# First feed-forward stage: input weights loaded and split first, every pair's front six chunks later, down products 12 chunks behind the up products

## The reference, cut to what matters

```python
xn = _layernorm(x, axis=-1)
gates = softmax(xt @ Wg.T); scores, inds = top_k(gates, 2); scores /= sum(scores)
g = einsum('td,ehd->teh', xt, We_gate)
u = einsum('td,ehd->teh', xt, We_up)
y_all = einsum('teh,edh->ted', silu(g) * u, We_down)
y = sum(take_along_axis(y_all, inds) * scores)
shared = silu(xt @ Ws_gate.T) * (xt @ Ws_up.T) @ Ws_down.T
y = y + sigmoid(xt @ Wsg.T) * shared
```

## Time and profile before

| what | us |
|---|---|
| median of three runs (lowest, highest) | 2506.7 (2501.7, 2507.82) |
| the profiled execution, its own time | 2507.11 |
| its span, first to last instruction | 2505.4 |
| TensorE busy (share of the span) | 2250.0 (90%) |
| VectorE busy | 1914.7 (76%) |
| ScalarE busy | 1736.3 (69%) |
| GpSimd busy | 843.7 (34%) |
| last instruction of the first stage | 424.5 |

### The profile page before, as it was taken

How to read it: one execution, slowest core, us unless ns; L and a number is a source line. 1 busy time by engine, 2 the same in 40 slices (tenths; PEclk the granted TensorE clock), 3 DMA queues, 4 the chain that set the end, 5 groups by cost and what they waited for, 6 DMA issues and landing times. The chain is left out here.

```text
span 2505.4 us, 90533 instructions
## 1 busy us (share of the span) xinstructions
PE 2250.0 (90%) x34464; PEld 1764.0 (70%) x34464; DVE 1914.7 (76%) x7571; ACT 1736.3 (69%) x5614; POOL 843.7 (34%) x911
## 2 busy tenths in 40 slices
PE   6999998799988899899899888779999699999998
PEld 5888887577777777777777676558777466666665
DVE  6777772567777778777777777658888588898888
ACT  2333332677777777777777777866666599999998
POOL 3666665020122211211112212221212556566562
PEclk9999999899999999999999999989999799999999
DMA  7857452666667666676667664013231111111110
GB/s 245 236 157 196 110 117 45 161 163 166 171 165 177 169 173 170 164 171 166 162 173 173 172 168 122 17 66 113 94 117 69 47 27 42 30 36 38 27 38 14
DMA packets 360772, 304.77 MB, mean 122 GB/s; under 512 B 25368, under 2 KB 328856, under 8 KB 358952
## 3 DMA queue, kind: packets, MB, share of 16 engines
q1 hardware_dynamic: 349864, 271.93, 42.6%
q0 software_dynamic: 10496, 27.28, 3.7%
HBM read 166.43 MB, written 132.69 MB: 119 GB/s over the span
## 5 line engine op out<-in xcount | busy, mean ns | idle before, releaser
L823 ACT ACTIVATE probs<-neg_scores,low 128x256 f32<-128x256 f32 (+1 forms) x1152 | 574.3, 500 | 244.2 <-DVE low L959 226.2
L959 DVE CUSTOM_DVE_ANT_0 neg_scores<-scores,rel_bias 128x256 f32<-128x256 f32 x1024 | 373.7, 421 | 244.3 <-PE scores L1121 126.7
L1135 PE MATMUL probsT<-consts,probs 128*128 128x128 f32 x2240 | 361.5, 284 | 54.2 <-ACT probsT_s L839 49.3
L1135 PEld LDWEIGHTS probsT<-consts,probs 128*128 128x128 f32 x2240 | 248.7, 142 | 111.8 <-ACT probsT_s L839 72.4
L774 POOL TENSOR_SCALAR q_heads<-q_raw,consts,q_bias 128x256 f32<-128x256 f32 x128 | 69.7, 558 | 746.6 <-ACT q_raw L805 746.5
L1685 DVE CUSTOM_DVE_ANT_0 neg_scores<-scores,alibi 128x128 f32<-128x128 f32 (+1 forms) x896 | 265.9, 352 | 57.4 <-PE scores L1741 53.5
L275 POOL TENSOR_TENSOR hid<-hid,gate_bc 128x512 f32<-128x512 f32 x160 | 205.7, 1291 | 151.9 <-DVE hid L448 141.9
L301 ACT ACTIVATE ga<-gate_up 128x512 f32<-128x512 f32 x160 | 95.6, 598 | 223.7 <-PE gate_up L514 208.5
L967 DVE COPY rel_s<-scores 128x768 f32<-128x768 f32 x256 | 244.0, 953 | 5.2 <-PE scores L1121 3.8
L1647 ACT ACTIVATE probs<-neg_scores,low 128x128 f32<-128x128 f32 (+1 forms) x448 | 199.6, 448 | 47.7 <-DVE low L1685 45.7
L1111 PE MATMUL scores<-k_sides,q_heads 32*128 32x256 f32 (+1 forms) x2304 | 205.5, 424 | 26.9 <-DVE rel_s L967 21.0
(11 more groups left out here) (205 smaller groups left out, 4942.6 us busy)
## 6 DMA issues: line engine op xcount, KB each, us to landing
rel_rows<-rel_s SPq DMA_DIRECT2D x256, 192.0 KB
rel_bias<-rel_rows SPq DMA_DIRECT2D x256, 192.0 KB, 3.4
gate_bc<-gate_rows SPq DMA_DIRECT2D x32, 1024.0 KB, 10.1
rel_rows<-rel_s SPq DMA_DIRECT2D x256, 128.0 KB
rel_bias<-rel_rows SPq DMA_DIRECT2D x256, 128.0 KB, 3.0
packed<-ffn_in SPq DMA_DIRECT2D x8, 1280.0 KB, 15.0
xe<-packed SPq DMA_DIRECT2D x16, 640.0 KB, 3.9
expert_out<-ye POOLq DMA_DIRECT2D x16, 640.0 KB, 3.2
```

Source lines behind the costliest of these rows:

```text
L823: act.activation(probs[s % 3][:, j, 0:w], neg[s % 2][:, j, 0:w], ACT.Exp, bias=low[s % 3][:, j:j + 1], scale=-1.0, accum_out=sums[s // UB ...
L959: dve.tensor_tensor_reduce(neg[s % 2][:, j, 0:w], S_ps[:, 512 * j:512 * j + w], bias_of(s)[:, j, :] if s < NU0 else alibi[:, 4 * j + s % 4 ...
L1135: ins = pe.transpose(PT_ps[:, j * P:(j + 1) * P], probs[u % 3][:, j, kt * P:(kt + 1) * P], ident)
```

## The change

The loads put `ffn_in` ahead of the weights and of x of pair 1. EARLY goes from 4 to -2, so that FIRST is -18: each place of each front is six steps later. LAG goes from 3 to 12. Among the places, GpSimd's output bias goes from 7 to 12 and VectorE's `lower_parts` from 13 to 10; GpSimd's wait for the rows goes from its start to the first bias. The semaphore of the down products is counted for every chunk, not every pair; VectorE's `hid` waits for the down products of the chunk whose buffer it takes; `add_ffn` runs two pairs behind at k = 3 instead of one pair behind at k = 4.

```diff
-            AHEAD, EARLY = 2, 4
+            AHEAD, EARLY = 2, -2
+            LAG = 12
...
                 sp.dma_start(consts[:, :], io["consts"]).then_inc(consts_in, 16)
+                sp.dma_start(ffn_in[:, :], io["ffn_in"]).then_inc(ffn_loaded, 16)
                 sp.dma_start(weights[:, :], io["weights"]).then_inc(weights_in, 16)
                 load_x(1)
-                sp.dma_start(ffn_in[:, :], io["ffn_in"]).then_inc(ffn_loaded, 16)
...
             def _(pool):
-                pool.wait_ge(rows_in, 16)
...
-                    new = front_pair(c, 7)
-                    if new is not None:
-                        pool.wait_ge(xn_done, new + 1)
-                        here = residual[:, TP * new:TP * (new + 1), :]
-                        pool.tensor_tensor(here, here, rview["bout"].unsqueeze(1).to_broadcast((P, TP, D)), ALU.add).then_inc(bout_added, 1)
...
+                    new = front_pair(c, 12)
+                    if new is not None:
+                        if new == 0:
+                            pool.wait_ge(rows_in, 16)
+                        pool.wait_ge(xn_done, new + 1)
+                        here = residual[:, TP * new:TP * (new + 1), :]
+                        pool.tensor_tensor(here, here, rview["bout"].unsqueeze(1).to_broadcast((P, TP, D)), ALU.add).then_inc(bout_added, 1)
...
                 def add_ffn(p):
-                    dve.wait_ge(down_done, p + 1)
+                    dve.wait_ge(down_done, NK * (p + 1))
...
-                        if k == 0 and p >= 2:
-                            dve.wait_ge(down_done, p - 1)
+                        if p >= 2:
+                            dve.wait_ge(down_done, s - 2 * NK + 1)
...
-                    if k == 4 and p >= 1:
-                        add_ffn(p - 1)
+                    if k == 3 and p >= 2:
+                        add_ffn(p - 2)
...
-                    if front_pair(s, 13) == 0:
+                    if front_pair(s, 10) == 0:
                         lower_parts()
...
+                add_ffn(NP - 2)
                 add_ffn(NP - 1)
...
-                    if k == NK - 1:
-                        ins.then_inc(down_done, 1)
-
-                LAG = 3
+                    ins.then_inc(down_done, 1)
```

## The result

The changed kernel takes 2550.8 us, the median of 4 runs (2540.5 to 2558.8), against 2507.3 us for the kernel before (4 runs, 2501.7 to 2508.7): ratio 1.0181, 95% interval 1.0157 to 1.0204. It is 43.6 us slower. Its profiled execution took 2549.4 us with a span of 2547.7, 42.3 us above the span before. So the loss is made in the stage that was changed; the stages behind it are 1.2 us shorter in this profile (2079.7 against 2080.9 us).

A forecast was written before the change was run, and what follows sets the result against it. TensorE was taken as the bound, busy 383.7 of 383.8 us. Ramp +1, pairs +38 and pair 14 +2 gave +41, less 2 is +39 on the median 2506.7: 2546 us, range 2514 to 2570 for 8 in 10.

The forecast's parts named there:

- Any new wait of TensorE in the other 384 us: First feed-forward stage after the ramp (40 to 423.8 us): TensorE is full, so any new wait adds its whole length.
- LAG, the semaphores and `add_ffn`: Down products 12 steps behind, finer semaphore counts, later `add_ffn`: work only moved or counted differently, so 0.
- The ramp, +1: Stage start: up product 0 5 us earlier, but later steps at VectorE's pace; net +1 us, ends -5 and +5.
- Each pair, +2.9: Every pair: GpSimd's run behind late gates holds VectorE's chain, TensorE waits; 27.5 us instead of 24.57, 38 over 13 pairs.
- L: Landing: when a pair's gates are in GpSimd's reach, counted from the pair's step 0; forecast 9.0 us.
- the zeros: Pair 2: gates come later still, behind 6.3 MB of zeros; 0 to 5 us, put into the range.
- The choice that L386, L397 and L399 would be held: VectorE's tensor-tensor instructions on SBUF, never seen held, taken as held by GpSimd; otherwise the first of two stalls goes.
- The smaller end, 2520: Every pair: only instructions of kinds already seen held are held, +1.05 us a pair, 2520 us in all.
- 2 off, since the first pairs aren't in the cycle yet: Sum of the terms: +41 us lowered by 2 to +39 for the first pairs.
- fit into VectorE's slack: Rival in every pair: holds fit VectorE's slack, TensorE stays full, only the ramp counts; -5 to 0, 2505 us, chance 0.15.
- VectorE did not become the bound: Rival in every pair: VectorE, held by twelve GpSimd instructions, becomes the bound; +6 x 14, 2590 us, chance 0.07.
- What would show it: Signs in the profile: TensorE some 2.9 us idle a pair, waits for `hid` and the gate broadcast, stage end near 463.

The follow-up runs named there:

- loads_only: The changed kernel with EARLY = 4, LAG = 3 and `add_ffn` of the pair before at k = 4: 2508.6 us, ratio 1.0017 to the kernel before.
- early4: The changed kernel with only the fronts put back to their old steps (EARLY = 4): 2517.9 us, ratio 1.0033 to the kernel before.
- early8_bunch: The changed kernel with EARLY = 8 and GpSimd waiting at each pair's first `hid` until four are ready: 2580.8 us, ratio 1.0271 to the kernel before.
- early8: The changed kernel with EARLY = 8, every place of the fronts ten steps earlier: 2526.4 us, ratio 1.0061 to the kernel before.

## Why the prediction came out right

*"Any new wait of TensorE in the other 384 us is paid in full."* Right: +43.5 us of stage, +42.3 of span.

*LAG, the semaphores and `add_ffn`: 0.* Right for each pair and at the tail (the down products run on to the end without a wait, as forecast, and `add_ffn` follows them by itself). Wrong for the ramp, by up to 6.3 us (`loads_only` against `early4`): I counted TensorE's work as moved, which it is, but not that it had also been the cover of the ramp's holds.

*The ramp, +1.* The gates at 40 (40.27), up product 0 at "about 23" (22.97), up product 10 at 46.1 (46.27) and up product 12 at 53 (52.00) came as worked out. The hand count stopped there, and the loss lies just behind it: from up product 12 to 13 (57.04) it is 5.04 us and from 13 to 14 (60.92) 3.88, where a step takes 2.28, 4.4 us more in both. This is the term that was mis-sized, about +5 for +1, inside the bounds of ±5. Two things in these steps were left out. VectorE's table preparations, in step 10, are held one by one (L418 at 52.53: 1.38 us), and `hid` 11, for which up product 13 waits 2.50 us, stands behind them. And TensorE fell to its lower level of 1.2 GHz: granted 0.82 from 52 to 60 us, three matmuls in 1.54 us at 57.04 instead of 0.94. It had fallen once before, behind the 3.96 us of standing (0.83 from 42 to 52 us, three matmuls in 1.48 us at 47.18 instead of 0.85), and the clearing held a half of `xn` (L365, 3.53 us for two); both lie ahead of up product 12, which came no later than forecast.

*Each pair, +2.9.* From 69.76 to 426.32 lie 13 periods of the gate transposes, 27.43 each against 24.57: +2.86, 37.2 us in all. With L at 10.0 after step 0 (197.22 - 187.23; 9.0 was forecast), up product 6 at 17.1 (16.9), stalls of 1.6 to 2.2 there (1.9), and 1.03 in sum at 8 and 9 (1.05): products 7, 8 and 9 start at 207.04, 210.08 and 212.63, 3.04 and 2.55 apart, that is 0.76 and 0.27 over 2.28. The remaining 6.3 of the 43.5 are product 6 of the first such pair, ahead of 69.76 (1.66), and the ramp, by difference about 4.6. In pair 2, where the zeros could cost up to 5, the gates came 11.1 us after step 0 (88.83 - 77.75) and the period was no longer than the others.

*The choice that L386, L397 and L399 would be held.* Right in kind: up to 1.33, 1.33 and 1.17 us where before they never were. But they are not all held in one pair: in seven pairs it is L397 (here L399), in the other seven the one-hot. And the chain is through sooner than worked out: up product 6 starts at L + 7.1 (204.31 - 197.22) and not at L + 7.9, while L itself is 1.0 us later than forecast. The two errors nearly cancel (17.1 for 16.9), so the close match at product 6 is partly luck. The smaller end, 2520 with only +1.05 a pair, would have been wrong. The rule of the Trainium skill that I weighed there ("GPSIMD Engine Reference", "1. Specifications"), two SBUF inputs contend, is borne out by L388, L399 and L401, which have two, and by `hid`, which reads PSUM and is never held.

*"2 off, since the first pairs aren't in the cycle yet".* Wrong, there was nothing to take off: pair 1 already stalls (1.66 at product 6, 67.38). The error of the sum, 2546 forecast and 2550.8 measured, is the ramp's +4 and these 2 us, less about one in the pairs.

*The rivals.* The holds do not fit into VectorE's slack when GpSimd runs back to back; they do when it is paced, where TensorE stays full, as that rival said of a broken-up run. VectorE did not become the bound: the run breaks after five, as worked out.

*What would show it.* Waits of TensorE for `hid` "about 28 times, 35 to 40 us": 30 times, 34.1. A wait in the trace is somewhat shorter than what it costs: up product 6 at 204.31 came 4.35 us after product 5 (199.96), 2.07 late, with a wait of 1.82. GpSimd for the broadcast "15 times, some 8 us": 16 times, 120.7, that is 6.4 each without the first (24.1). Stage end "near 463": 468.0.

## What to carry to other kernels

An engine that waits for late data and then catches up in a run is not the same as one that is merely late: look at what its burst does to its neighbours. Here a wait added to GpSimd, so that it stays five steps behind VectorE, took 40 us off. And before you take slack from one engine (LAG) or move work out of a ramp, ask which waits that work was hiding.

## What the runs showed of the hardware that was not expected

Unlinked neighbours are held as well: L398 takes 1.26 us at 199.83 beside one GpSimd instruction (0.16 us at 120.37, alone), though it needs no result that is late. Held instructions pass at the boundaries between GpSimd's: linked ones one at each, unlinked ones sometimes two (L396 ends at 199.85 and L397 at 199.92, at the one boundary of 199.82). GpSimd's clearing, which only writes (2.23 us at 41.51), comes in the 3.53 us in which the two instructions of L365 run.

The Trainium skill ("SBUF — State Buffer", section "Who interferes with whom") describes the shared ports as a lock for a whole instruction, which a tensor_scalar can also want in a two-port mode. These rows agree with it.

TensorE's clock fell after one wait of 3.96 us (0.83 granted) and, in `early8_bunch`, under stalls of 2.74 to 3.23 us every pair (0.94 granted from 60 to 400 us), though the matmuls behind them were slow in every second pair only. In the changed kernel, with stalls of up to 2.2 us a pair, it was granted 1.00 over the same stretch. There a stall cost its own length; in `early8_bunch` 35.5 us of waits came with some 17 us of slower work. In the ramp of `early8` a wait of 2.11 us was already followed by three matmuls of 1.65 us, and at 197.04 in `early8_bunch` one of 2.74 us by three of 0.98, so the length of the stall alone doesn't decide it.
